# Start of a two-layer flamingo kernel: the first token group's chain and the linear weights ahead, keys and projection weights inside rounds 2 to 4

## The chip, the cores and the metric

One core of a Trainium2 chip runs one program. The metric is the device time of an execution in microseconds (us). One more execution was taken with the hardware profiler; its rows are what is read here. Engines: TensorE (PE; its weight loads are PEld), VectorE (DVE), ScalarE (ACT), GpSimd (POOL) and SyncE (SP), which only issues DMAs.

## The reference, cut to what matters

x is 4 x 2048 tokens of 512 values (8192 tokens), ctx 4 x 77 of 512. All in float32.

```
x = x + tanh(g) * memory(ctx, layernorm(x))     # shifted tokens; 19 "compressed" rows per batch:
                                                # conv_w (4 taps, stride 4) over 76 normed rows of x[1024:1100]
x = x + tanh(g) * (mxq(layernorm(x)) @ mxq(w).T + b)     # blocks of 32, 6-bit grid
x = x + tanh(g) * attention(layernorm(x), keys = D * relu(ctx @ U.T), values = ctx, key mask)
x = x + tanh(g) * experts(layernorm(x))         # router over 8 experts, capacity 1280, relu MLP 512-2048-512
```

The compressed rows enter as the tokens of the last quarter tile of group 1 of each batch. Key mask, keys, values and the router's logits of the context are made once, before they are used.

## The kernel before

Tokens are worked in 16 groups of 512 (4 tiles of 128 rows). A software pipeline of six stages runs over them: in round t the call `body(*groups(t))` on every engine has z = t, a = t-1, b = t-2, c = t-3, d = t-4, e = t-5, each a group's number or None. z: statistics and scale of the first layer norm (`moments("a")`, then `a_m`, `a_sc`, `nb` on VectorE; GpSimd scales `xs` at L1128). a: GpSimd adds `xs` to `X` (L1101), second statistics (L1660), ScalarE normalises to `n1` (L1198), VectorE quantises to `q8` (L1857 to L1869), GpSimd multiplies back (L1112) and adds `gbias` to `X` (L1121), TensorE turns the tiles (`turn_quantised`, L1413), ScalarE and VectorE split them into a high and a low part (`xdT_hi`, `xdT_lo`). b: the linear product with `wd_hi`, `wd_lo` (`linear`, L1405), its addition (L1717), turned tiles of X. c: projection with `uw_hi`, `uw_lo` (L1483), logits, product with the keys (`p_cs`). d: softmax and attention, router. e: slots and stores. Every float32 product is three passes over high and low parts.

Rounds 0 to 5 are written out, rounds 6 to 15 are a loop on the engines that have one, the rest is written out again. The expert stage follows, and its code isn't touched.

The order on each engine is that of its program; the waits on semaphores `k_dve`, `k_act`, `k_pe` go by the place of a step in the lists `DVE_STEPS`, `ACT_STEPS` and `PE_STEPS` (L287 to L303). Preparations: `xc` (76 rows of each batch) is normed and turned (`xcT`), the four taps of `conv_w` are multiplied (L1589), `comp` is stored in `comp_d` and read back as part of group 1's `xs` (L988). `wf` (linear weights) is quantised by VectorE (L1994 to L2002) and multiplied back by GpSimd (L1165), then turned and split (`wd`). `uf` (key weights) is centred by ScalarE with its row sums (L1365 to L1371), turned and split (`uw`). `cx` (the context) is turned and split (`cxT`), and stored split (`cx_d`). Keys: L1618 on TensorE, three steps a part on VectorE (L2009 to L2014), split (L1388, L2042) and stored (`uq_d`). Logits of the context: L1631.

Before the change all preparations but those of `xc` stand between round 0 and round 1 on TensorE, ScalarE and VectorE. GpSimd does the context's low parts (L1161) and `wf` (L1165) ahead of round 0. SP issues the loads in the order g, xc, four taps, group 0 (`load_group`), biases, wf, uf, cx, small ones; then `comp_d`, group 1, the stores of `cx_d` and `uq_d`, waits for everything (`prepared`, `stored`), and goes on with the keys and group 2. `load_group` waits for the addition L1101 of the group before, since `xs` is one buffer.

Of the kernel before, what the change touches and what calls it, by code (L numbers as in the profile page):

```python
# [18 lines left out]
F32 = mybir.dt.float32  # L19
# [9 lines left out]
P = 128  # L29
# [7 lines left out]
def flamingo_two_layers(nc, x, ctx, kmask, g_xattn, g_ffn, conv_w, conv_b, ffn_w, ffn_b, u_w, d_param,  # L37
# [45 lines left out]
    with top:  # L83
# [154 lines left out]
        with setup:  # L238
# [3 lines left out]
            uf = st("uf", [P, KB, D], F32)  # L242
            us, umean, unm = st("us", [P, KB], F32), st("umean", [P, KB], F32), st("unm", [P, KB], F32)
# [3 lines left out]
            xc = st("xc", [CW, B, D], F32)  # L247
            wq8 = st("wq8", [P, KB, D], FP8)
            xcT = st("xcT", [P, KB, B * CW], F32)
# [11 lines left out]
            zrow = n1[0:1, 1, :]  # L261
            comp = n1[0:B * TC, 0, :]
# [11 lines left out]
            uqf = X[:, 2 * T:3 * T, :].rearrange("p t d -> p (t d)")[:, 0:KB * B * L].rearrange("p (k l) -> p k l", k=KB)  # L274
# [3 lines left out]
            l_gate, l_small, l_wf, l_uf, l_cx, l_xc, l_wr = (sem("l_" + n) for n in  # L278
                                                             ("gate", "small", "wf", "uf", "cx", "xc", "wr"))
# [6 lines left out]

            DVE_STEPS = ["zero", *[f"xst{b}" for b in range(B)], *[f"xmv{b}" for b in range(B)],  # L287
                         *[f"xn{b}" for b in range(B)], "nmask", "ng", "mg", *[f"xcT{k}" for k in range(KB)],
                         "gbias", "kmf", "kfree",
                         "wab", "wsc", "win", "wq8", "comp", *[f"uw{k}" for k in range(KB)],  # L290
                         *[f"cxT{k}" for k in range(KB)], *[f"uq{w}{k}" for k in range(KB) for w in "maf"],
                         *[f"wd{k}" for k in range(KB)], "anyk", "anyi", "anyr", "gx", "kbias", "maskb", "wrc", "wrlo", "cwf", "cwlo",
                         *[f"uqlo{k}" for k in range(KB)]]
            dve_at = {n: i + 1 for i, n in enumerate(DVE_STEPS)}
            PE_STEPS = [*[f"xcT{k}" for k in range(KB)], "comp", *[f"uw{k}" for k in range(KB)],
                        *[f"cxT{k}" for k in range(KB)], "keysum", "wrsum", *[f"uq{k}" for k in range(KB)],
                        *[f"wd{k}" for k in range(KB)], "anyk", "cwr"]
            pe_at = {n: i + 1 for i, n in enumerate(PE_STEPS)}
            ACT_STEPS = ["xln", "xrs", "onesr", *[f"us{k}" for k in range(KB)], "unm", "umean", *[f"uc{k}" for k in range(KB)],
# [33 lines left out]
        def convolved(eng):  # L333

            for s, value in ((k_pe, pe_at["comp"]), (w_comp, 16), (w_init, 48)):
                eng.wait_ge(s, value)
# [1808 lines left out]
```

## Time and profile before

| | us |
|---|---|
| median of 3 runs (lowest, highest) | 2067.8 (2064.79, 2069.31) |
| the profiled execution, its time | 2065.28 |
| its span, first to last instruction | 2063.5 |
| TensorE busy in the span | 1927.6 (93%) |
| VectorE, ScalarE, GpSimd busy | 964.2, 742.2, 757.6 |
| mean granted TensorE clock | 0.97 |

The token stage takes the first 700 us or so of the span, the experts the rest. A busy share is an average over both; what the change touches is the first 170 us, read below row by row. The number behind a row's start is its length or that of the merged pieces; x is their count; in square brackets stands the engine's idle time ahead of it and what ended it. A window's row has its stretch, its length, then busy time and instruction count of PE, PEld, DVE, ACT and POOL, the granted TensorE clock (1.00 is 2.4 GHz, 0.50 is 1.2 GHz), the busy share of the DMA queues and GB/s.

### The profile page before, as it was taken

To read this page: it belongs to the slowest core of one execution; us is meant where nothing else is said; L and a number is where in the kernel's file an instruction comes from. 1 tells how busy PE (TensorE), PEld (TensorE's weight loads), DVE (VectorE), ACT (ScalarE), POOL (GpSimd) and SP (SyncE) were. 2 spreads that over 40 slices of the span, in tenths; PEclk is the share of its full clock that TensorE was granted. 3 is DMA by queue.
4 is the path that set the end of the run, shared out by engine and by line. 5 is a ranking of instruction groups with operands and counts; after the bars stand their busy time and mean duration, and the time that the engine had idled before them with its cause. 6 is when DMAs were issued, how large, how long until landed. Compare 5 with 4: busy or idle time off the path is not lost.

```text
span 2063.5 us, 34727 instructions
## 1 busy us (share of the span) xinstructions
PE 1927.6 (93%) x10956; PEld 1637.0 (79%) x10957; DVE 964.2 (47%) x2254; ACT 742.2 (36%) x1707; POOL 757.6 (37%) x803
## 2 busy tenths in 40 slices
PE   3579999999999739999999999999999999999997
PEld 2467777777777538989889988998898898899986
DVE  3678999999996571423312241224224124122331
ACT  2235666666566531423311141114214114111231
POOL 0456566675664231423311151115215115211340
PEclk9589999999999869999999999999999999999999
DMA  7231453443544381433401152004305115200220
GB/s 199 93 94 42 142 178 119 167 136 125 182 133 161 106 284 31 145 96 94 130 30 30 36 167 66 30 30 153 98 25 173 36 36 168 77 30 30 81 82 11
DMA packets 152268, 208.77 MB, mean 101 GB/s; under 512 B 12830, under 2 KB 78622, under 8 KB 152197
## 3 DMA queue, kind: packets, MB, share of 16 engines
q1 hardware_dynamic: 111125, 114.14, 17.8%
q0 software_dynamic: 15728, 43.38, 7.0%
q10 hardware_dynamic: 25344, 50.33, 6.8%
q8 instruction: 41, 0.67, 0.1%
q14 instruction: 30, 0.25, 0.0%
HBM read 140.98 MB, written 68.37 MB: 101 GB/s over the span
## 4 chain that ended last, share of the span: by engine, by line
PE 78%; DVE 6%; issue 5%; DVEq 1%; DMA 1%; ACT 1%; POOL 1%; SPq 0%; ACTq 0%; POOLq 0%
PE bank L788 25%; PE bank L796 24%; PE bank L1483 7%; PE bank L1405 6%; PE bank L756 6%; PE bank L736 6%; PE bank L1455 1%; DVE x2T_lo L1803 1%; PE bank L714 1%; PE bank L745 1%; DVE xdT_lo L1803 1%; DMA stage<-in_L_ffn_W_dram 1%; PE bank L1413 1%; DVE up_lo L1794 1%; DVE a_m L1899 0%
## 5 line engine op out<-in xcount | busy, mean ns | idle before, releaser
L896 DVE SCALAR_TENSOR_TENSOR hT_lo<-bank,hT_hi 128x256 fp32r<-128x256 f32 x352 | 149.2, 424 | 676.9 <-ACT hT_hi L664 676.9
L664 ACT ACTIVATE hT_hi<-bank 128x256 fp32r<-128x256 f32 x352 | 134.9, 383 | 753.9 <-PE bank L788 753.9
L788 PE MATMUL bank<-inT_hi,w_hi 128*128 128x256 f32 x1408 | 399.7, 284 | 0.6 <-DVEq L944 0.6
L788 PE MATMUL bank<-inT_hi,w_lo 128*128 128x256 f32 x1408 | 400.0, 284 | 0.0
L788 PE MATMUL bank<-inT_lo,w_hi 128*128 128x256 f32 x1408 | 396.7, 282 | 0.0
L796 PE MATMUL bank<-w_hi,hT_hi 128*128 128x512 f32 x704 | 280.8, 399 | 0.0
L796 PE MATMUL bank<-w_lo,hT_hi 128*128 128x512 f32 x704 | 277.9, 395 | 0.0
L788 PEld LDWEIGHTS bank<-inT_lo,w_hi 128*128 128x128 f32 x1408 | 266.3, 189 | 14.5
L796 PE MATMUL bank<-w_hi,hT_lo 128*128 128x512 f32 x704 | 277.6, 394 | 0.0
L788 PEld LDWEIGHTS bank<-inT_hi,w_hi 128*128 128x128 f32 x1408 | 266.0, 189 | 13.9 <-DVEq L944 1.0
L788 PEld LDWEIGHTS bank<-inT_hi,w_lo 128*128 128x128 f32 x1408 | 265.2, 188 | 0.0
L497 POOL TENSOR_TENSOR w_lo<-stage,w_hi 128x512 fp32r<-128x512 f32 x112 | 163.4, 1468 | 104.4 <-ACT w_hi L624 104.2
L502 POOL COPY idx_t<-slots 128x2 int32 x23 | 4.2, 184 | 537.5 <-PE bank L714 524.3
L796 PEld LDWEIGHTS bank<-w_hi,hT_lo 128*128 128x128 f32 x704 | 132.2, 188 | 31.9
L796 PEld LDWEIGHTS bank<-w_hi,hT_hi 128*128 128x128 f32 x704 | 132.7, 189 | 17.3
L796 PEld LDWEIGHTS bank<-w_lo,hT_hi 128*128 128x128 f32 x704 | 132.9, 189 | 15.9
L861 DVE TENSOR_TENSOR w_lo<-stage,w_hi 128x512 fp32r<-128x512 f32 x128 | 119.0, 943 | 0.0
L1405 PE MATMUL bank<-wd_hi,xdT_hi 128*128 128x512 f32 x256 | 105.1, 411 | 4.7 <-DVE xdT_lo L1803 2.7
L1483 PE MATMUL bank<-x2T_hi,uw_hi 128*128 128x512 f32 x256 | 106.0, 414 | 1.0 <-DVE rpe L1739 1.0
L1090 POOL TENSOR_SCALAR y<-x,y_sc,y_nb 128x512 f32<-128x512 f32 x64 | 49.4, 785 | 141.7 <-DVE y_nb L1764 141.6
L1405 PE MATMUL bank<-wd_hi,xdT_lo 128*128 128x512 f32 x256 | 101.2, 395 | 0.0
L1405 PE MATMUL bank<-wd_lo,xdT_hi 128*128 128x512 f32 x256 | 101.0, 395 | 0.0
(314 smaller groups left out, 3830.5 us busy)
## 6 DMA issues: line engine op xcount, KB each, us to landing
stage<-in_L_ffn_W_dram SPq DMA_DIRECT2D x256, 256.0 KB, 3.2
X<-in_x_dram SPq DMA_DIRECT2D x16, 1024.0 KB, 5.5
t_d<-tt ACTq DMA_DIRECT2D x16, 1024.0 KB, 4.4
x_d<-x ACTq DMA_DIRECT2D x16, 1024.0 KB, 6.7
out_dram<-y ACTq DMA_DIRECT2D x16, 1024.0 KB, 8.4
xs<-in_x_dram SPq DMA_DIRECT2D x16, 768.0 KB
cw_a<-in_L_xattn_conv_w_dram SPq DMA_DIRECT2D x2, 1024.0 KB, 17.8
cw_b<-in_L_xattn_conv_w_dram SPq DMA_DIRECT2D x2, 1024.0 KB, 19.9
```

What stands on the lines that cost most here:

```text
L497: pool.tensor_tensor(w1_lo[:, :, fs], w1_block(f), w1_hi[:, :, fs].bitcast(F32), ALU.subtract).then_inc(e_split[f % RING], 1)
L664: act.activation(hT_hi[:, f % 4, :], hb[f % 4][:, 0:CN], ACT.Relu).then_inc(e_hh, 1)
L736: last = pe.matmul(first_bank[q % 2][:, :], l[:, k, :], r[:, k, qs], start=(n == 0), stop=(n == 3 * KB - 1))
L756: last = pe.matmul(unit_acc[:, :], l[:, q % 2, f, :], r[:, q * FQ + f, :], start=(q == 0 and n == 0), stop=(q == NF - 1 and n == 3 * FQ - 1))
L788: last = pe.matmul(hb[f % 4][:, 0:CN], l[:, k, fs], r[:, k, :], start=(n == 0), stop=(n == 3 * KB - 1))
L796: last = pe.matmul(acc[i][:, :], l[:, f % 4, js], r[:, f, :], start=(f == 0 and n == 0), stop=(f == FB - 1 and n == 2))
L861: dve.tensor_tensor(w2_lo[:, f, :], w2_block(f), w2_hi[:, f, :].bitcast(F32), ALU.subtract).then_inc(e_split[f % RING], 1)
L896: dve.scalar_tensor_tensor(out=hT_lo[:, f % 4, :], in0=hb[f % 4][:, 0:CN], scalar=0.0, in1=hT_hi[:, f % 4, :].bitcast(F32), op0=ALU.max, o ...
L1090: pool.tensor_scalar(y[:, j:j + 1, :], x3[:, ds((g % 2) * T + j, 1), :], y_sc[:, j:j + 1], y_nb[:, j:j + 1], ALU.mult, ALU.add).then_inc(g ...
L1405: last = pe.matmul(dst, l, r, start=(n == 0), stop=(n == len(terms) - 1))
L1483: last = pe.matmul(u_banks[h % 2][:, :], l, rows_t, start=(k == 0 and n == 0), stop=(k == KB - 1 and n == 2))
L1803: dve.tensor_tensor(lo[:, :, j * P:j * P + P], banks[j % len(banks)][:, :].rearrange("p (k i) -> p k i", k=KB), hi[:, :, j * P:j * P + P]. ...
```

## The change

Loads: xc is read in two pieces (rows 0 to 63, 64 to 75), then tap 0, group 0, tap 1, wf, tap 2, uf, tap 3, the biases with a semaphore of their own (`l_bias`), cx in two pieces, the small ones. Group 2 is fetched right behind group 1, group 3 behind the stores of context and keys. TensorE: the turned linear weights `wd` stand between taps 2 and 3; `uw` behind `comp`; `cxT` (three banks instead of four) between rounds 1 and 2; keys inside round 2, ahead of the turned tiles of group 1; the context's logits inside round 3. VectorE: `wf` after round 0; `gbias`, `comp` and the `wd` low parts inside round 1; mask, `uw` and `cxT` between rounds 1 and 2; key steps inside round 2, their low parts and the small steps behind it; `cwf` inside round 3. In round 1 the first statistics of group 1 come behind the turned tiles. ScalarE: row sums of `uf` ahead of round 1; `wd`, centring and `uw` inside it. GpSimd: rounds start at once; `wf` inside round 1 behind the addition to X, the context's low parts inside round 2. Buffers: `comp`, `xcT`, `wq8`, `uqf` lie in parts of `X` that are free so long. The blanket waits `convolved`, `prepared` and `stored` are gone, single ones take their place. `first_moments` and `first_scale` are the two pieces that stood in VectorE's body before. The core of the diff, banks and list orders left out:

```diff
+            def load_taps(r):
                 half_r = (cw_a, cw_b)[r // (RATE // 2)]
                 sp.dma_start(half_r[:, r % (RATE // 2), :, :], cwv[r, :, :, :]).then_inc(l_cw[r], 16)
+
+            for s0, s1 in ((0, P // 2), (P // 2, CW)):
+                sp.dma_start(xc[s0:s1, :, :], x[:, HALF + s0:HALF + s1, :].rearrange("b s d -> s b d")).then_inc(l_xc, 16)
+            load_taps(0)
             load_group(0, 0)
-            sp.dma_start(fb_raw[:, :], row(ffn_b).broadcast_to([P, D])).then_inc(l_small, 16)
-            sp.dma_start(cb_raw[:, :], row(conv_b).broadcast_to([P, D])).then_inc(l_small, 16)
+            load_taps(1)
             sp.dma_start(wf[:, :, :], ffn_w.rearrange("(k p) i -> p k i", p=P)).then_inc(l_wf, 16)
+            load_taps(2)
             sp.dma_start(uf[:, :, :], u_w.rearrange("(k p) i -> p k i", p=P)).then_inc(l_uf, 16)
-            sp.dma_start(cx[:, :, :], ctx.rearrange("b l d -> l b d")).then_inc(l_cx, 16)
+            load_taps(3)
+            sp.dma_start(fb_raw[:, :], row(ffn_b).broadcast_to([P, D])).then_inc(l_bias, 16)
+            sp.dma_start(cb_raw[:, :], row(conv_b).broadcast_to([P, D])).then_inc(l_bias, 16)
+            for l0, l1 in ((0, P // 2), (P // 2, L)):
+                sp.dma_start(cx[l0:l1, :, :], ctx[:, l0:l1, :].rearrange("b l d -> l b d")).then_inc(l_cx, 16)
...
+            for r0, r1 in ((0, P // 2), (P // 2, B * TC)):
+                sp.dma_start(comp_d[r0:r1, :], X[r0:r1, 3 * T, :]).then_inc(w_comp, 16)
+            sp.wait_ge(w_comp, 32)
             load_group(0, 1)
+            load_group(0, 2)
             sp.wait_ge(k_cxlo, B)
...
+            sp.wait_ge(k_act, act_at[f"uqhi{KB - 1}"])
             sp.wait_ge(k_dve, dve_at[f"uqlo{KB - 1}"])
             sp.dma_start(uq_d.rearrange("b p c -> p b c"),
                          uq_hl[:, :, :, :, :].bitcast(F32).rearrange("p b w k l -> p b (w k l)")).then_inc(w_uq, 16)
-            prepared(sp)
-            stored(sp)
+            sp.wait_ge(w_cx, 16)
+            sp.wait_ge(w_uq, 16)
             load_keys(0)
-            load_group(0, 2)
+            sp.wait_ge(w_init, 48)
             load_group(0, 3)
...
+            def weight_dequantised():
+                pool.wait_ge(k_dve, dve_at["wq8"])
...
+                pool.wait_ge(k_dve, dve_at["gbias"])
+
+            body(*groups(0))
+            body(*groups(1), beside=weight_dequantised)
+            body(*groups(2), beside=context_low)
+            pool.wait_ge(w_init, 48)
+            for t in range(3, STEPS - 1):
...
+            def centred_and_linear():
+                for k in range(KB):
+                    act.wait_ge(k_pe, pe_at[f"wd{k}"])
+                    act.activation(wd_hi[:, k, :], bank[bank_of[f"wd{k}"]][:, :], ACT.Copy).then_inc(k_act, 1)
+                for k in range(KB):
+                    act.activation(uf[:, k, :], uf[:, k, :], ACT.Identity, bias=unm[:, k:k + 1]).then_inc(k_act, 1)
+                act.wait_ge(k_pe, pe_at["comp"])
+
+            def projection_high():
+                for k in range(KB):
+                    act.wait_ge(k_pe, pe_at[f"uw{k}"])
+                    act.activation(uw_hi[:, k, :], bank[bank_of[f"uw{k}"]][:, :], ACT.Copy).then_inc(k_act, 1)
+
+            body(*groups(1), beside=(centred_and_linear, projection_high))
...
+            body(*groups(2))
...
+            body(*groups(3))
...
+                if r == RATE - 1:
+                    pe.wait_ge(k_wdq, KB)
+                    for k in range(KB):
+                        transposes(f"wd{k}", [(slice(n * P, n * P + P), wf[:, n, k * P:k * P + P]) for n in range(KB)])
                 pe.wait_ge(l_cw[r], 16)
...
+            pe.wait_ge(k_dve, dve_at["wd1"])
+            body(*groups(1))
+            pe.wait_ge(l_cx, 32)
+            for n in range(CXN):
+                pe.wait_ge(k_dve, dve_at[("wd2", "wd3", "uw0")[n]])
...
+            def keys():
...
+            def context_logits():
...
+            body(*groups(2), beside=keys)
+            body(*groups(3), beside=context_logits)
...
+                if beside is not None:
+                    beside()
+                opening = isinstance(a, int) and a == 0
+                if not opening:
+                    first_moments()
                 turned_rest(q_banks, xdT_hi, xdT_lo, a, 0, a_bh, v_bl)
                 turned_rest(q_banks, xdT_hi, xdT_lo, a, 1, a_bh, v_bl)
                 up_rest(2)
...
+                if not opening:
+                    first_scale()
                 up_rest(3)
                 turned_rest(q_banks, xdT_hi, xdT_lo, a, 2, a_bh, v_bl)
                 turned_rest(q_banks, xdT_hi, xdT_lo, a, 3, a_bh, v_bl)
+                if opening:
+                    first_moments()
+                    first_scale()
...
+            def compressed_and_linear():
+                dve.wait_ge(l_bias, 32)
+                step("gbias", dve.tensor_scalar(gbias[:, :], fb_raw[:, :], gates[:, 2:3], None, ALU.mult))
+                dve.wait_ge(k_pe, pe_at["comp"])
+                step("comp", dve.tensor_tensor(comp, bank[7][0:B * TC, :], cb_raw[0:B * TC, :], ALU.add))
+                for k in range(KB):
+                    low_part(f"wd{k}", wd_lo[:, k, :], wd_hi[:, k, :])
+
+            body(*groups(1), beside=compressed_and_linear)
+            dve.wait_ge(l_small, 32)
+            step("kmf", dve.tensor_copy(kmf[:, :], km[:, :]))
+            after("kmf")
+            step("kfree", dve.tensor_scalar(kfree[:, :], kmf[:, :], -1.0, 1.0, ALU.mult, ALU.add))
+            for k in range(KB):
+                low_part(f"uw{k}", uw_lo[:, k, :], uw_hi[:, k, :])
+            for n in range(CXN):
+                low_part(f"cxT{n}", cx_turned(cxT_lo, n), cx_turned(cxT_hi, n))
...
+            def keys():
+                for h in range(KB):
+                    dve.wait_ge(k_pe, pe_at[f"uq{h}"])
...
+            body(*groups(2), beside=keys)
...
+            def context_logits():
+                dve.wait_ge(k_pe, pe_at["cwr"])
...
+            body(*groups(3), beside=context_logits)
```

## Rows read from the trace of the kernel before

**Rows 1.** Windows: busy and count per engine, granted clock, DMA share, GB/s

```profile
0.00:20.00 20.00, 0.00 (x0) 0.01 (x1) 3.39 (x11) 3.29 (x6) 2.32 (x20) 1.00 0.84 209
104.00:108.00 4.00, 3.35 (x8) 2.70 (x9) 1.10 (x2) 0.00 (x0) 4.00 (x5) 0.50 0.14 48
200.00:240.00 40.00, 40.00 (x209) 31.37 (x208) 37.36 (x107) 26.19 (x64) 28.17 (x29) 1.00 0.40 132
```

**Rows 2.** Timeline of TensorE: taps, context logits, first linear product of round 4

```profile
25.07 8.55 PE L1589 MATMUL bank<-cw_a,xcT 128*76 128x512 f32 x16 [0.57 <-DVE xcT L1985]
...
78.67 0.30 PE L1631 MATMUL bank<-wr_hl,cxT_hi 128*77 128x16 f32 x1 [2.89 <-DVE wr_hl L2035]
...
82.72 0.28 PE L1631 MATMUL bank<-wr_hl,cxT_lo 128*77 128x16 f32 x1
...
167.62 0.39 PE L1405 MATMUL bank<-wd_hi,xdT_hi 128*128 128x512 f32 x1
```

**Rows 3.** Timeline of GpSimd: dequantisation, scale, additions of groups 0 to 2

```profile
63.56 4.06 POOL L1165 TENSOR_TENSOR wf<-wq,wsc 128x512 f32<-128x512 fp8e4 x4
67.60 3.15 POOL L1128 TENSOR_SCALAR xs<-xs,a_sc,nb_a 128x512 f32<-128x512 f32 x4
70.92 5.19 POOL L1101 TENSOR_TENSOR X<-X,xs 128x512 f32<-128x512 f32 x4 [0.17 <-issue]
...
108.28 5.02 POOL L1101 TENSOR_TENSOR X<-X,xs 128x512 f32<-128x512 f32 x4 [0.17 <-issue]
...
137.34 5.04 POOL L1101 TENSOR_TENSOR X<-X,xs 128x512 f32<-128x512 f32 x4 [0.17 <-issue]
```

**Rows 4.** Timeline of SP: issue of group 1's compressed rows

```profile
77.03 3.75 SPq L988 DMA_DIRECT2D xs<-comp_d  x1
```

**Rows 5.** Timeline of ScalarE: row sums of uf, centring, group 0 normalised

```profile
42.52 0.63 ACT L1365 ACTIVATE uf<-uf 128x512 f32<-128x512 f32 x1 [7.55 <-DMA uf<-in_L_xattn_U_w_dram]
...
45.35 2.56 ACT L1371 ACTIVATE uf<-uf,unm 128x512 f32<-128x512 f32 x4
...
88.88 2.92 ACT L1198 ACTIVATE n<-X,nb_b,rs_b 128x512 f32<-128x512 f32 x4 [0.23 <-DVE nb_b L1670]
```

**Rows 6.** Windows as rows 1, four stretches of the load phase

```profile
20.86:33.83 12.97, 11.28 (x33) 5.96 (x34) 5.69 (x15) 0.00 (x0) 0.00 (x0) 1.00 1.04 336
6.00:15.00 9.00, 0.00 (x0) 0.00 (x0) 0.00 (x0) 0.00 (x0) 0.00 (x0) 1.00 1.04 224
16.50:22.00 5.50, 0.08 (x1) 0.11 (x2) 4.80 (x14) 0.50 (x2) 0.00 (x0) 1.00 1.05 387
36.00:45.00 9.00, 4.49 (x11) 1.92 (x9) 0.00 (x0) 2.48 (x8) 0.00 (x0) 1.00 0.43 101
```

**Rows 7.** Timeline of VectorE: statistics and scale, wf, keys, their low parts, q8

```profile
31.40 2.47 DVE L1660 BATCH_NORM_STATS2 st_a<-xs 128x6 f32<-128x512 f32 x4 [6.39 <-DMA xs<-in_x_dram]
...
35.29 0.15 DVE L1902 SCALAR_TENSOR_TENSOR nb_a<-mv_a,a_m 128x4 f32<-128x4 f32 x1
...
45.78 2.27 DVE L1994 TENSOR_REDUCE wab<-wf 128x64 f32<-128x2048 f32 x1
...
48.91 2.29 DVE L2002 TENSOR_TENSOR wq<-wf,win 128x2048 fp8e4<-128x2048 f32 x1
...
65.76 0.54 DVE L2009 TENSOR_SCALAR X<-bank,umean 128x308 f32<-128x308 f32 x1 [7.29 <-PE bank L1618]
...
73.37 0.38 DVE L2014 TENSOR_SCALAR X<-X,dp 128x308 f32<-128x308 f32 x1
...
83.66 1.64 DVE L2042 TENSOR_TENSOR uq_hl<-X,uq_hl 128x308 fp32r<-128x308 f32 x4
...
93.49 2.50 DVE L1869 TENSOR_TENSOR q<-n,i 128x512 fp8e4<-128x512 f32 x4
```

**Rows 8.** Waits of SP: engine, line, releaser: us in total, times, longest

```profile
SPq L347 <- DMA cx_d<-cx_hl: 10.5, 1, 10.5
...
SPq L98 <- DMA comp_d<-n: 2.9, 1, 2.9
```

More of the change, by code:

```diff
@@ L291, in flamingo_two_layers @@
[L291 to L293 removed]
+                         "wab", "wsc", "win", "wq8", "gbias", "comp", *[f"wd{k}" for k in range(KB)], "kmf", "kfree",
+                         *[f"uw{k}" for k in range(KB)], *[f"cxT{n}" for n in range(CXN)],
@@ L1332, in body @@
                 quantised_hi(3)
+                if beside[1] is not None:
+                    beside[1]()
+                if z is not None and opening:
+                    rstd("a", z)
                 for j in range(T):
@@ L1555, in body @@
                 turn_logits()
+                if beside is not None:
+                    beside()
                 turn_quantised(0)
@@ L1616, in _ @@
+            def keys():
+                pe.wait_ge(k_act, act_at["onesr"])
+                pe.wait_ge(k_dve, dve_at[f"cxT{CXN - 1}"])
                 for k in range(KB):
-                    for n, (a, c) in enumerate(((uw_hi, cxT_hi), (uw_hi, cxT_lo), (uw_lo, cxT_hi))):
-                        last = pe.matmul(bank[bank_of[f"uq{h}"]][:, 0:B * L], a[:, k, hs], c[:, k, :],
-                                         start=(k == 0 and n == 0), stop=(k == KB - 1 and n == 2))
+                    for c in (cxT_hi, cxT_lo):
+                        last = pe.matmul(bank[bank_of["keysum"]][:, 0:B * L], onesr[:, :], c[:, k, :],
+                                         start=(k == 0 and c is cxT_hi), stop=(k == KB - 1 and c is cxT_lo))
@@ L1628, in _ @@
-            for b in range(B):
-                for k in range(KB):
-                    for part in (cxT_hi, cxT_lo):
-                        last = pe.matmul(cwr_bank[:, b, :], part[:, k, b * L:b * L + L], wr_hl[:, k, :],
-                                         start=(k == 0 and part is cxT_hi), stop=(k == KB - 1 and part is cxT_lo),
-                                         skip_group_check=True)
-            last.then_inc(k_pe, 1)
-            body(*groups(1))
-            prepared(pe)
-            for t in range(2, STEPS):
+                pe.wait_ge(l_wr, 16)
@@ new lines, in context_logits @@
+            def context_logits():
+                for b in range(B):
+                    for k in range(KB):
+                        for part in (cxT_hi, cxT_lo):
+                            last = pe.matmul(cwr_bank[:, b, :], part[:, k, b * L:b * L + L], wr_hl[:, k, :],
+                                             start=(k == 0 and part is cxT_hi), stop=(k == KB - 1 and part is cxT_lo),
+                                             skip_group_check=True)
+                last.then_inc(k_pe, 1)
```

276 lines of the change are left out of this document (118 added, 158 removed).

## The prediction

> **What bounds the kernel now.** I read the busy time by stretch first. In a full round the TensorE is busy 40.00 of 40.00 us at the full clock [rows 1]. From there on the order of work is unchanged by the edit, and nothing in it is tied to an absolute time, so it can only start earlier or later as a whole. The question is therefore when the first full round starts: the TensorE begins the linear product of group 2, which opens round 4, at 167.62 us [rows 2]. Second, the chain before it. The rounds cannot start before GpSimd turns to the tokens: it does the context's low parts and then the weight dequantisation (63.56 to 67.62) first, then scales group 0's tokens (67.60) and adds them to X (70.92 to 76.11) [rows 3], though their statistics were there long before. Group 1's tokens are fetched only after that addition: the third piece is issued at 77.03 [rows 4]. So each of rounds 1 to 3 is a loop of latencies (load, statistics, GpSimd scale 3.2, add 5.2, statistics, normalise, quantise, turn), with one addition per round, ending at 76.1, 113.3 and 142.4 [rows 3], and the TensorE is idle in much of it. Third, the load phase: all engines wait for DMA until about 42.5, when the key weights land and ScalarE starts on them [rows 5].
>
> **The loads.** They are put in order of need, and xc and cx are cut at partition 64. In the old order the aggregate was 224 GB/s from 6 to 15 us with xc in flight, 387 after it, 336 over the middle, and 101 at 0.43 of the queues' time over 36 to 45, where cx is the tail [rows 6]. Up to and with uf the new order holds 608 + 3 x 1024 (taps 0 to 2) + 1024 (xs) + 1024 (X) + 1024 (wf) + 1024 (uf) = 7776 KB, 7.96 MB. About 2.3 MB go by 15 us (the old rate from some 4.5 us on); 5.6 MB at 336 GB/s take 16.8, so 31.8, and I add 1.2 for landing: **uf at 33**, against 42.5. Bounds: 31 at 387 GB/s, 36 if the slow start lasts longer. By the same count wf lands at 27, tap 2 at 30, tap 3 at 36, the group-0 tokens at 18 and their X at 21. The Trainium skill (DMA: Bandwidth & Descriptors, "Why a DMA increments its semaphore by 16 and not by 1") says that a transfer runs on the largest number of engines up to 16 that divides its outer dimensions; 76 rows give 4 engines and 77 give 11, while 64 give 16. The tail's share of 0.43 leans that way. If the rule were void, xc would land about where it did, and the sum below would not move, since uf sets it.
>
> **Group 0.** Its statistics, scale and X addition take place at about 18 to 30 (scale 3.2, addition 5.2 [rows 3]), beside the wait for wf and uf. VectorE then does the weight quantisation, 45.78 to 51.20 before, so 5.4 [rows 7]: 27 to 32.4, and group 0's second statistics, about 3 more. ScalarE's row sums and means of uf take 42.52 to 45.35 = 2.8 [rows 5], and they stand ahead of round 1 on its queue: 33 + 2.8 = 35.8 is later than VectorE's 35.4, so uf is what ends last. Add 0.9 for rstd and shift: normalising starts at 36.7. From its start to the end of q8 it was 88.88 to 95.99 = 7.1 [rows 5, 7]: **q8 done at 43.8**, against 95.99. The wait of GpSimd for gbias costs 0.5, with the dequantised tiles of n1 queued behind it.
>
> **Compressed memory and group 1.** comp follows on VectorE, at 45.0, if the TensorE has tap 3 by then: dequantisation 32.4 + 4.1 = 36.5 [rows 3], four wd transposes about 3, a tap 4.3 (half of 8.55 [rows 2]) = 43.8. It would be 48 to 50 at the low clock. Then the store, 2.9 [rows 8] plus 0.3, and the fetch of group 1: in the old run from the end of the addition (76.11) the third piece's issue ran to 80.78 [rows 3, 4], and I take 7 us with the landing (5 to 9): **xs of group 1 at 55.2**. This is a new wait on VectorE's queue, with uw_lo, cxT_lo and round 2 behind it; the TensorE's cxT of the last bank waits too. Statistics, rstd and scale took 31.40 to 35.44 = 4.0 for group 0 [rows 7], GpSimd 3.2 and 5.1, and some 0.5 between them: addition done at **68** against 113.3 [rows 3], 45 earlier. Splits of uw and cxT (about 4 us of VectorE) lie beside GpSimd's 8 and cost nothing; without that cover they would cost those 4.
>
> **Round 2.** The first linear product starts after uw_lo 0, at about 62, and its first tile at the low clock (8 records of 512 columns in 4 us, 0.5 granted [rows 1]) ends at 67; statistics of group 1 thus end at 70.6, not 69, the fourth tile at 75.4. Reduction and q8 need 6 more: **82**, against 125, 43 earlier. Now the keys: 65.76 to 73.75 on VectorE, 8.0 [rows 7], ahead of group 2's statistics and of every low part of the turned tiles. The TensorE makes them from 75.4 to 85, so they overlap and are fed in time. Of the 8, about 5 to 6 count in the end, since the statistics and scale of group 2, which used to run beside GpSimd's bias addition and were slowed by it, now come after it. Scale done at 94.4, GpSimd 3.2 and 5.1: addition of group 2 done at **102.6** against 142.4 [rows 3], 39.8 earlier. Bounds of this step: 4 to 9 lost.
>
> **Round 3.** Key low parts (1.64 [rows 7]) and about ten mask steps of 128 x 16 and less, together an estimated 3.4, stand before round 3 on VectorE. They lie partly beside GpSimd's addition (8 us with the scale), but the low parts of the turned tiles fill most of that, and the linear product again begins at the low clock, which puts group 2's statistics behind it by 2 to 3. I take 4.8 lost (2 to 8): 35 left. The context logits take 78.67 to 83.00 = 4.3 on the TensorE [rows 2], ahead of the turned tiles, and VectorE's reduction of them stands ahead of group 3's statistics; here the TensorE is busy without a gap, so all of it counts. **30.6 left; round 4 opens at 137.0** instead of 167.62. The key store is issued at about 102. In the old run it went out behind the context store, for which alone SP waited 10.5 [rows 8]; alone, and as large (1232 KB each), I take 8 (4 to 17), so group 3's tokens, now behind it on SP, land near 118 (114 to 127), against a need at 127. Hidden, just so at the upper end. The removed waits (convolved, prepared, stored) save nothing: they stood after their work.
>
> **The clock.** The window 0 to 20 shows the full clock granted with no matmul in it, and 104 to 108 the low one, 1.2 GHz, after an idle stretch of the TensorE [rows 1]. The Trainium skill (TensorE: Matmul & The Clock Gate, "What's actually happening") has the throttled state as the default after idling. By that rule, which speaks against this change because it spreads the TensorE's preparations over waits, all taps run at half speed. That is rival B.
>
> **Sum.** Profiled execution: span 2063.5, time 2065.3, so 1.8 lies around it; 2065.3 - 30.6 = 2034.7. The median of the three runs is 2.5 above the profiled one; with half of that, **2036**.
>
> **Rivals.** A, more is gained: loads run at 387 GB/s (uf at 31), the keys cost 4 and the store is quick: 2 + 2 + 3 more, 2029; down to 2023 if group 1's fetch takes 5 and the uw, cxT and mask steps are all covered. For it: the 387 [rows 6]. Against it: the same table's slow start, whose cause no row shows.
> B, low clock in the preparations: three taps behind each other cost 4.3 more each [rows 2], the wd transposes 3; comp comes at 51 instead of 45, and the first linear products lose 2 to 5 more. 8 to 12 of the gain go: 2044 to 2048. Against it: the window 0 to 20 has 1.00 granted with the TensorE idle throughout, and the old taps followed at 0.53 a record [rows 1, 2]; for it: new gaps of 2 to 3 us between taps that wait for DMA.
> C, a new wait takes the place of the old one: group 1's fetch after comp, or group 3's behind the key store. The first decides at once, 1 us per us above 55.2; with landing at 62 it is 2043. The second decides from 127 on; with the store at 17 and the fetch slowed by the X load 5 to 8 are lost: 2042.
> D, no change: the round trips only move, that is, round 4 still opens at 165 to 170. Groups 1 to 3 would have to lose 30 us; [rows 3] show 37 us of addition-to-addition time between groups 0 and 1, and 29 between 1 and 2. I don't see it. 2065.
> E, slower: the TensorE stays at the low clock from round 2 until the first full round. Its work there is about 250 records (two groups' linear products 96, keys and key sums 56, projection and logits 56, the rest turned tiles), at 0.19 us each (40 us for 209) 48 us; at the low clock it doubles (0.43 to 0.5 a record there [rows 1]). Of 48 us more some 12 go into idle time: 2036 + 36 = 2072. It decides once more than 31 + 12 of the 48 are run at the low clock, less it is only B. Against it: the old run had the same kind of gaps and the low clock at 104 to 108, and yet opened round 4 62 us later.
>
> **Chances.** Forecast (2028 to 2041): 0.55. A (below 2028): 0.13. B and C with gains of 4 to 24 (2041 to 2061): 0.24. D: 0.04. E: 0.04. The range 2023 to 2053 leaves out D, E, and the ends of A and B. A measurement of this kernel tells 0.2%, 4.1 us, from no change: faster 0.92, same 0.04, slower 0.04.
>
> **What would show it.** Right: uf's row sums start near 33; the addition of group 1 ends near 68 and of group 2 near 103 on GpSimd; VectorE waits some 4 us for group 1's tokens, and never for group 3's; keys stand between q8 and the statistics of group 2; the linear product of group 2 opens at 137; everything after has the old spacing. Wrong: uf later than 36; a granted clock of 0.5 in the taps; a DMA as what ended the wait for group 3's statistics; or full rounds that are no longer 40 of 40.

## The result and the profile after

The changed kernel takes 2040.3 us (median of 4 runs, 2039.7 to 2042.1) against 2066.7 of the kernel before, run beside it: ratio 0.9872, 95% interval 0.9858 to 0.9886. It is faster by 26.4 us; 2036 was forecast, so the time is 4.3 us longer, inside the forecast range of 2028 to 2041 and near its upper end. The profiled execution took 2040.0, with a span of 2038.2 (25.3 less than before) and a mean granted clock of 0.977 for 0.970.

Timeline of TensorE: start, length, engine, line, what; in brackets the idle time ahead and what ended it. These lines answer to [rows 2].

```profile
16.70 8.63 PE L1625 MATMUL bank<-cw_a,X 128*76 128x512 f32 x16 [0.57 <-DVE X L2036]
25.91 3.73 PE L1625 MATMUL bank<-cw_b,X 128*76 128x512 f32 x8 [0.59 <-DMA cw_b<-in_L_xattn_conv_w_dram]
35.08 3.68 PE L1606 MATMUL bank<-ident,wf 128*128 128x128 f32 x16 [5.44 <-POOL wf L1174]
38.55 4.47 PE L1625 MATMUL bank<-cw_b,X 128*76 128x512 f32 x8
...
128.59 0.23 PE L1667 MATMUL bank<-wr_hl,cxT_hi 128*77 128x16 f32 x1
...
130.83 1.09 PE L1439 MATMUL bank<-ident,n 128*128 128x128 f32 x8
...
142.07 0.51 PE L1431 MATMUL bank<-wd_hi,xdT_hi 128*128 128x512 f32 x1 [1.67 <-DVE cwr L2109]
```

Round 4 opens at 142.07 for 167.62, 25.55 earlier, and this is the whole gain: the addition to X of group 15 ends at 589.4 for 614.8, 25.4 earlier, and the spacing of one group's addition to the next is 37.2 in both traces (two neighbouring groups: 291.1 - 253.9 and 316.8 - 279.6). So the question is again what set 142.07.

Timeline of GpSimd, which answers to [rows 3]: the additions end at 31.0, 75.0, 108.2 and 144.5 for 76.1, 113.3, 142.4 and 172.1, that is 45, 38, 34 and 28 earlier. Each round of the three gives some of the start back.

```profile
24.02 7.00 POOL L1105 TENSOR_TENSOR X<-X,xs 128x512 f32<-128x512 f32 x4 [0.17 <-issue]
30.98 4.05 POOL L1174 TENSOR_TENSOR wf<-X,wsc 128x512 f32<-128x512 fp8e4 x4
...
69.98 5.05 POOL L1105 TENSOR_TENSOR X<-X,xs 128x512 f32<-128x512 f32 x4 [0.17 <-issue]
...
102.67 5.52 POOL L1105 TENSOR_TENSOR X<-X,xs 128x512 f32<-128x512 f32 x4 [0.28 <-POOL xs L1134]
```

Timeline of VectorE, which answers to [rows 7]. The third line holds its largest wait of the first 150 us.

```profile
8.08 2.47 DVE L2019 BATCH_NORM_STATS2 xst<-xc 76x6 f32<-76x512 f32 x4 [6.55 <-DMA xc<-in_x_dram]
16.56 2.46 DVE L1698 BATCH_NORM_STATS2 st_a<-xs 128x6 f32<-128x512 f32 x4
62.52 2.47 DVE L1698 BATCH_NORM_STATS2 st_a<-xs 128x6 f32<-128x512 f32 x4 [12.72 <-DMA xs<-comp_d]
...
84.78 2.50 DVE L1929 TENSOR_TENSOR q<-n,i 128x512 fp8e4<-128x512 f32 x4
...
104.41 4.51 DVE L2083 TENSOR_TENSOR uq_hl<-X,uq_hl 128x308 fp32r<-128x308 f32 x4
...
141.28 0.74 DVE L2109 TENSOR_TENSOR cwr<-cwf,cwr 77x32 fp32r<-77x32 f32 x1 [0.92 <-ACT cwr L1422]
```

What the 12.72 are: the first line is the chain that ended last (start, length, what), the others are windows, with the columns of [rows 1].

```profile
47.29 15.09 DMA xs<-comp_d
...
54.00:57.00 3.00, 0.00 (x0) 0.00 (x0) 0.00 (x0) 0.00 (x0) 0.00 (x0) 0.50 0.78 266
57.00:60.00 3.00, 0.00 (x0) 0.00 (x0) 0.00 (x0) 0.00 (x0) 0.00 (x0) 0.50 0.07 25
60.00:62.50 2.50, 0.00 (x0) 0.00 (x0) 0.00 (x0) 0.00 (x0) 0.00 (x0) 0.50 0.07 25
```

From 57 us on nothing in the core works but the DMA engines, and they at 0.07 of the time of all sixteen and 25 GB/s: about one of the sixteen carries what is left. The fetch of group 1 has pieces of 768 KB (384 rows), 218 KB (109 rows) and 38 KB (19 rows), and X of 1024 KB. This gave the experiments.

### The profile page after: what moved, and what is told of

Same layout as the page of the kernel before. It is cut to its first block, busy times and chain, and to the rows that moved or that the text cites. A ratio compares the mean times of both kernels' runs of the same rounds, so it can differ in the third digit from the quotient of the medians.

```text
span 2038.2 us, 34720 instructions
## 1 busy us (share of the span) xinstructions
PE 1918.6 (94%) x10956; PEld 1629.3 (80%) x10957; DVE 960.5 (47%) x2253; ACT 741.8 (36%) x1706; POOL 760.7 (37%) x803
## 4 chain that ended last, share of the span: by engine, by line
PE 82%; DVE 7%; issue 5%; DMA 2%; DVEq 1%; ACT 1%; POOL 1%; ACTq 0%; SPq 0%; POOLq 0%
PE bank L781 25%; PE bank L789 24%; PE bank L1511 7%; PE bank L1431 7%; PE bank L729 6%; PE bank L749 6%; PE bank L1483 1%; DVE x2T_lo L1841 1%; PE bank L707 1%; PE bank L738 1%; DMA xs<-comp_d 1%; DVE xdT_lo L1841 1%; PE bank L1439 1%; DVE a_m L1860 0%; DVE up_lo L1832 0%
## 6 DMA issues: line engine op xcount, KB each, us to landing
cw_a<-in_L_xattn_conv_w_dram SPq DMA_DIRECT2D x2, 1024.0 KB, 10.8
```

## The experiments

All kernels compute the full reference. Each was run beside the kernel before; the times (in us), and the start of round 4 in the one execution that was profiled:

| kernel | median us | ratio to before (95%) | round 4 opens |
|---|---|---|---|
| changed kernel | 2040.3 | 0.9872 (0.9858, 0.9886) | 142.07 |
| e1_split | 2032.0 | 0.9834 (0.9818, 0.9851) | 134.80 |
| e2_early | 2034.4 | 0.9847 (0.9831, 0.9864) | 135.04 |
| e7_order | 2029.7 | 0.9821 (0.9805, 0.9838) | 130.97 |
| e5_xcwhole | 2048.6 | 0.9908 (0.9892, 0.9925) | 150.71 |
| e6_tapsfirst | 2046.5 | 0.9901 (0.9885, 0.9918) | 149.16 |
| e4_uqlo | 2038.2 | 0.9869 (0.9852, 0.9885) | 140.81 |
| e8_keysact | 2039.7 | 0.9865 (0.9849, 0.9882) | 141.65 |
| e10_keysact_uqlo | 2034.9 | 0.9847 (0.9830, 0.9863) | 137.67 |
| e3_cwlo | 2038.4 | 0.9869 (0.9852, 0.9885) | 141.12 |
| e9_warm | 2040.6 | 0.9875 (0.9859, 0.9892) | 140.75 |
| e11_best | 2021.3 | 0.9779 (0.9763, 0.9795) | 124.11 |
| e12_best_g3 | 2022.6 | 0.9781 (0.9764, 0.9797) | 124.86 |

The intervals are some 3 us to either side, so smaller differences between two of these kernels are not told apart by them; for those I go by the start of round 4 in the trace. That has a scatter too: six of the kernels (the changed one, e3_cwlo, e4_uqlo, e8_keysact, e9_warm, e10_keysact_uqlo) fetch group 1 in the same way, and its statistics start between 61.7 and 62.7 in their traces. About 1 us in the start of round 4 is therefore no effect of an edit by itself.

### Group 1's fetch

**e1_split** cuts the odd piece of every group's fetch; in group 1 its 109 rows become 96 and 13.

```diff
-                sp.dma_start(xs[0:m, T - 1, :], rows(r + shift + G - P, m)).then_inc(s_xs, 16)
+                cut = {1: 96, 3: 48}.get(q, P // 4)
+                for m0, m1 in ((0, cut), (cut, m)):
+                    sp.dma_start(xs[m0:m1, T - 1, :], rows(r + shift + G - P + m0, m1 - m0)).then_inc(s_xs, 16)
```

> Every group's fetch goes in four pieces instead of three: the first piece, of 109 rows in groups 1, of 51 in groups 3 and of 64 in the others, is cut into 96+13, 48+3 and 32+32 rows. In the changed kernel group 1's tokens reach VectorE at 62.5 us, 15.5 us after SyncE issued them, and from 60 to 65 us the DMA engines' share is .06, one engine of sixteen. Theory: the tail is the 109-row piece that one engine carries. Then 96 rows spread, 13 rows are a short tail, the statistics of group 1 start at 54 to 57 and round 4's first matmul comes 5 to 7 us earlier, at 135 to 137; the time is 2033 to 2036. Rival: the compressed rows (19, written to DRAM and read back, not cut here) or the round trip of their store hold the group; then the statistics still start at 61 to 63 and the time stays at 2039 to 2042.

Measured: 2032.0. VectorE's statistics, then the chain that ended last:

```profile
54.20 2.47 DVE L1700 BATCH_NORM_STATS2 st_a<-xs 128x6 f32<-128x512 f32 x4 [4.49 <-DMA xs<-comp_d]
...
47.78 6.29 DMA xs<-comp_d
```

8.3 us earlier, with the same bytes, in one piece more. The theory holds (the time is 1 us better than its range); the 19 rows and their way through DRAM were not what held the group. SyncE's issue of the compressed rows, 4.01 us long in the changed kernel, took 0.25 here: it too had waited behind the piece of 109 rows. The rule behind it was in the prediction for another load. The Trainium skill (DMA: Bandwidth & Descriptors, "Why a DMA increments its semaphore by 16 and not by 1") picks the largest number of engines up to 16 that divides the outer dimensions; by that rule 109 gives one engine and 96 gives sixteen, and the trace agrees, with 0.07 of sixteen engines' time at 25 GB/s behind the 109 rows.

**e2_early** moves everything of group 1 but the 19 rows ahead of the wait (`late=True` leaves these out).

```diff
+            load_group(0, 1, late=True)
             sp.wait_ge(k_dve, dve_at["comp"])
...
-            load_group(0, 1)
+            sp.dma_start(xs[KEEP_A - (HALF - P):P, T - 1, :], comp_d[0:TC, :]).then_inc(s_xs, 16)
```

> Of group 1's fetch, everything but the 19 compressed rows (its 109 other token rows and X) is issued ahead of SyncE's wait for the compressed rows; only the 19 rows follow the store. Theory: VectorE's 12.7 us of idle time ahead of group 1's statistics is the transfer of the large piece, which has no reason to wait. Then the statistics start at 50 to 53, the addition to X of group 1 ends by 65, and round 4's first matmul comes 8 to 10 us earlier; 2030 to 2033. First rival: the store and read back of the 19 rows, on one engine, take over, so that the statistics start at 56 to 58 and the gain is 4 to 6 us (2034 to 2036). Second rival: what is late next (GpSimd's scales and additions, TensorE's first linear layer at 68 with its clock low before it) takes nearly all; round 4 opens within 2 us of 142 and the time is 2038 to 2042.

Measured: 2034.4, the time of the first rival (its statistics at 56 to 58 are missed). The large piece is out of the way, and yet the statistics start at 54.34. SyncE's waits (engine, line, releaser: us in total, times, longest), then windows of the stretch before and during this wait:

```profile
SPq L1049 <- DMA comp_d<-X: 6.2, 1, 6.2
```

```profile
40.00:42.00 2.00, 2.00 (x6) 1.04 (x5) 1.58 (x3) 1.84 (x4) 0.21 (x1) 1.00 0.95 337
42.00:44.00 2.00, 2.00 (x15) 1.50 (x15) 1.12 (x2) 0.00 (x0) 2.00 (x3) 1.00 0.24 84
...
46.00:48.00 2.00, 0.96 (x8) 0.82 (x9) 1.29 (x2) 0.95 (x3) 2.00 (x2) 1.00 0.07 25
```

SyncE waited 6.2 us for the store of the compressed rows, for 1.4 in the changed kernel. I first put this down to X's 1 MB, now in flight ahead of the store, and the expectation of the next run says so. The windows show something else. The bulk of the loads was through by 43, and the store was issued at 43.59; from 46 on the engines are at 0.07 and 25 GB/s again, the mark of the 109 rows, which are not cut in this kernel. What fits is a store held up by the queue of one engine: the odd piece, and X's share on that engine behind it. That is read from the windows and not shown by a run, and how the 6.2 us split between the two is not measured. **e7_order** takes both away: it has both edits, and X behind the compressed rows:

> Both ideas on group 1's fetch together, with one more: the 109-row piece is cut as in the kernel with four pieces (96+13), all of the group's token rows are issued ahead of SyncE's wait for the compressed rows, and X follows only behind the 19 compressed rows. Where only the rows and X went early, the store of the compressed rows took 6.2 us, with X's 1 MB in flight, and the statistics of group 1 started at 54.3. Theory: the store was held up by X; without it the store takes about 2.5 us, the 19 rows some 3, and the statistics start as soon as VectorE is free, at 49.6 to 51. TensorE's and GpSimd's work of round 1 ends at 49.5 and 50.8, so round 4's first matmul comes 3 to 4.5 us ahead of the 134.8 of the kernel with four pieces: 130.5 to 132; 2029 to 2031. Rival: the 19 rows' way through DRAM, on one engine, takes the same 6 us however empty the queues are; the statistics start at 53 to 54 and the time is 2032 to 2034.

Measured: 2029.7, the theory in time and in the start of round 4; its reason, that X alone held the store, is not shown by it, since the odd piece is cut in it as well.

```profile
50.33 2.47 DVE L1704 BATCH_NORM_STATS2 st_a<-xs 128x6 f32<-128x512 f32 x4 [0.75 <-DMA xs<-comp_d]
...
130.97 0.50 PE L1437 MATMUL bank<-wd_hi,xdT_hi 128*128 128x512 f32 x1 [1.69 <-DVE cwr L2115]
```

SyncE's wait for the store is 1.4 us again, and of VectorE's 12.72 us of waiting 0.75 are left. From the changed kernel to this one the statistics come 12.2 earlier, round 4 11.1, the span 10.8. In e1_split it is 8.3, 7.3 and 5.2: there round 4 had the low clock soon after its start, as these windows show, and gave some back.

```profile
136.00:138.00 2.00, 2.00 (x6) 1.58 (x5) 0.00 (x0) 0.00 (x0) 0.00 (x0) 0.50 0.35 48
138.00:140.00 2.00, 2.00 (x10) 1.57 (x10) 0.27 (x1) 0.00 (x0) 0.00 (x0) 0.75 0.88 327
```

### The loads

**e5_xcwhole** undoes the cut of xc alone (`for s0, s1 in ((0, CW),)`), **e6_tapsfirst** the order alone (`load_taps(0)` to `load_taps(3)` ahead of `load_group(0, 0)`).

> Of the change, only the cut of the compressed segments' load is undone: the 76 rows come in one piece and not in 38 and 38; the order of the loads stays that of the changed kernel. In the kernel before VectorE started on these rows at 16.5, in the changed one at 8.1. Theory: with one piece, on a few of the sixteen engines, the rows arrive at 14 to 16 again; VectorE makes them before group 0's statistics, which then start at 21 to 24 for 16.6, and all that follows shifts by 5 to 7 us: 2045 to 2047. Rival: the pieces behind it gain from the engines that it leaves free, and group 0's chain has slack up to the linear weight at 23.2: 2040 to 2042.

> The order of the loads is that of the kernel before: all four convolution taps, then group 0's tokens, the linear weight, the projection weight; all else is as in the changed kernel. Theory: in the changed kernel the linear weight (VectorE starts on it at 23.2, after 2.6 us of idle time) and group 0's tokens (16.6) set round 1; with 2 MB of taps ahead of the tokens, 5 to 6 us at 387 GB/s, group 0's statistics start at 21 to 23 and the linear weight lands at 28 to 29; the normalised tokens come 4 to 5 us later, tap 3 waits for nothing more than before, and the time is 2043 to 2045. Rival: the last tap matmul and the projection weight, whose place in the queue hardly moves, set the compressed rows and with them group 1's fetch; the time stays at 2040 to 2041.

(The change cuts xc into 64 and 12 rows; the 38 and 38 of the first text are a slip.) Measured: 2048.6 and 2046.5; both theories, each some 1.5 us above its upper end. The first two lines are of e5_xcwhole, the third is of e6_tapsfirst:

```profile
16.37 2.47 DVE L2019 BATCH_NORM_STATS2 xst<-xc 76x6 f32<-76x512 f32 x4 [14.84 <-DMA xc<-in_x_dram]
...
24.84 2.46 DVE L1698 BATCH_NORM_STATS2 st_a<-xs 128x6 f32<-128x512 f32 x4
```

```profile
23.58 2.47 DVE L1696 BATCH_NORM_STATS2 st_a<-xs 128x6 f32<-128x512 f32 x4 [6.84 <-DMA xs<-in_x_dram]
```

Against 16.56 group 0's statistics come 8.3 and 7.0 later, and the addition of group 0 ends 8.3 and 7.0 later too (39.3, 38.0 for 31.0); the medians are 8.3 and 6.2 up. There is next to no slack behind group 0's statistics: what they lose, the kernel loses. Nearly a third of the change's 26.4 hangs on the cut of a 608 KB load.

### VectorE and GpSimd beside each other

**e4_uqlo** moves the keys' low parts into round 3, just ahead of VectorE's last linear addition, away from GpSimd's addition of group 2.

```diff
+                if between is not None:
+                    between()
                 add_linear(3)
```

> The low parts of the projected keys (one VectorE subtraction of 4.51 us at 104.4 in the changed kernel, 1.64 us in the kernel before) stand inside round 3, just ahead of VectorE's third linear addition, in place of ahead of the first. Theory: the operation is long because GpSimd runs an addition of the same kind beside it, and there it holds round 3's linear additions up. In its new place VectorE has some 2 us to spare and GpSimd is quiet: it lasts 1.6 to 1.7 us, and round 4 opens 3 to 4.5 us earlier; 2036 to 2037.5. Rival 1: the length is the operation's own in this layout; it stays 4.5 and costs 2 to 3 us at its new place: 2038.5 to 2040. Rival 2: the stores of the keys and group 3's fetch behind them come later by some 10 us, land at about 137 or later, and hold round 3's last statistics: slower, 2041 to 2046.

Measured: 2038.2, round 4 at 140.81: 1.3 us gained, and not the 3 to 4.5. The operation itself did as the theory says (1.65, first line). The rest went into what the second line shows, group 3's tokens, which now stand behind the keys' store, and into GpSimd's addition, which ended at 108.1 as before: two of the small steps now stand beside it, and took 0.85 and 1.23 us (`anyr`, `gx`) for 0.16 and 0.23. So rival 2 holds in part.

```profile
113.27 1.65 DVE L2107 TENSOR_TENSOR uq_hl<-X,uq_hl 128x308 fp32r<-128x308 f32 x4
...
129.87 2.47 DVE L1698 BATCH_NORM_STATS2 st_a<-xs 128x6 f32<-128x512 f32 x4 [1.19 <-DMA xs<-in_ctx_dram]
```

**e8_keysact** gives four of the keys' twelve operations to ScalarE.

```diff
-                    step(f"uqm{h}", dve.tensor_scalar(uqf[:, h, :], bank[bank_of["keysum"]][:, 0:B * L], umean[:, h:h + 1],
-                                                      None, ALU.mult))
-                    after(f"uqm{h}")
+                    dve.wait_ge(k_act, act_at[f"uqs{h}"])
...
+                for k in range(KB):
+                    act.activation(uqf[:, k, :], bank[bank_of["keysum"]][:, 0:B * L], ACT.Copy,
+                                   scale=umean[:, k:k + 1]).then_inc(k_act, 1)
```

> The product of the keys' column sums with the projection's means (four operations of 0.53 us on VectorE inside round 2) is made by ScalarE, which stands idle there for 4.8 us; VectorE's part of the keys, 87.2 to 94.8 in the changed kernel, shrinks to some 5.4 us. Theory: VectorE is busy without a gap from 81.4 to 100 in round 2, so what the keys take on it counts in full: 2.1 to 2.4 us less, round 4's first matmul at 139.7 to 140, 2037.5 to 2038.5. Rival: GpSimd's scale and addition of group 2 or TensorE's transpositions stand beside the keys and take their place: less than 0.8 us is gained, 2039.5 to 2041.

Measured: 2039.7, round 4 at 141.65: the rival. But its reason is another one. The keys shrank from 7.6 to 4.1 us (87.63 to 91.7) and round 3's first product came 3.0 earlier, at 99.58. Then:

```profile
96.41 1.19 DVE L1870 TENSOR_TENSOR a_sc<-a_m,ng 128x4 f32<-128x4 f32 x1
...
101.26 5.97 DVE L2089 TENSOR_TENSOR uq_hl<-X,uq_hl 128x308 fp32r<-128x308 f32 x4
...
109.21 0.65 PE L1439 MATMUL bank<-wd_hi,xdT_hi 128*128 128x512 f32 x1 [3.92 <-DVE X L1763]
```

VectorE ran into all of GpSimd's addition (101.18 to 106.90). Its four subtractions and GpSimd's four additions took turns, at some 1.5 us for each of the four pairs; TensorE stood 3.9 us and then had the low clock. **e10_keysact_uqlo** has both edits:

> Two edits together on the changed kernel, each of which has run alone: the keys' four mean products on ScalarE, and the subtraction for the keys' low parts inside round 3. With ScalarE's products alone round 3 opened 3.0 us earlier (99.6 for 102.6), but that subtraction then lasted 5.97 us for 4.51, TensorE stood 3.9 us and fell to the low clock, and round 4 opened only 0.4 us earlier. Theory: the gain was real and was lost in the contention of VectorE and GpSimd; with the subtraction away from GpSimd's addition the two gains add up to more than their sum, round 3's second statistics end at 108 to 109 (113.1 in the changed kernel), round 4 opens at 137 to 139; 2035 to 2036.5. Rival: GpSimd's addition to X of group 2 itself, or group 3's tokens, issued behind the store of the keys and needed 15 us after it, hold the round in their turn: round 4 opens at 140 or later, 2037.5 to 2039.

Measured: 2034.9, round 4 at 137.67: 4.4 earlier, where the two edits alone gave 1.3 and 0.4. In this execution group 1's fetch came 0.8 earlier; even without that the two together give more than their sum. The theory holds, and the 4.51 us of the low parts were contention.

How it works is seen in the smallest operations: a_sc, 128 x 4 values, takes 0.16 us where GpSimd is idle. In e8_keysact it started at 96.41, 0.11 us behind one of GpSimd's additions (96.30 to 97.58), took 1.19 and ended with it. Not every operation is slowed. In the changed kernel group 2's statistics, which read one tile in SBUF, took 2.46 us beside GpSimd's additions as elsewhere, and the key step with an operand in PSUM (the memory that TensorE writes to; here `bank`) 0.48. The Trainium skill (SBUF — State Buffer, "SBUF: two separate sides") has VectorE and GpSimd share a pair of ports, which VectorE needs for an operation with two inputs in SBUF or in a two-port mode, and which whoever comes first holds for its whole instruction; by that rule such an operation waits for the rest of GpSimd's running instruction, whatever its own size, and this trace agrees.

### The waits and the clock

**e3_cwlo** moves TensorE's wait for `cwlo` into round 4, to its use, and ScalarE's part of the step into round 3.

> TensorE's wait for the low part of the context logits' weight, which stands ahead of round 4, stands at the first use of that weight inside round 4, and ScalarE makes the high part inside round 3 and not behind it. Theory: in the changed kernel TensorE's 1.67 us of idle time ahead of round 4 is this wait and nothing else; round 4's first matmul then comes 1.7 us earlier, at 140.4, and the time is 2038.5. Rival: the wait only covers for VectorE's or ScalarE's own lateness, and the same idle time turns up a few instructions later in round 4: 2040.

Measured: 2038.4, as the theory has it; but round 4 opens at 141.12 and not 140.4. The wait of 1.7 us is gone (no idle time ahead of round 4), the context logits had begun 0.4 us earlier (128.21 for 128.59), and the clock took 1.1 back: a low spell stands right behind the context logits where the changed kernel has none.

```profile
130.00:132.00 2.00, 2.00 (x18) 1.98 (x18) 1.37 (x4) 0.71 (x2) 2.00 (x3) 0.77 0.00 0
132.00:134.00 2.00, 2.00 (x6) 1.54 (x5) 2.00 (x8) 0.86 (x3) 2.00 (x2) 0.50 0.00 0
```

TensorE's work just before it, the context logits, is the same in both. So a gain of 1 to 2 us in these rounds can be taken or given by where such a spell falls; what decides it the rows don't show.

**e9_warm** keeps TensorE busy while it has nothing to do.

```diff
+                if n == 2:
+                    pe.wait_ge(v_bl, T)
+                    for _ in range(70):
+                        pe.matmul(bank[2][:, :], xdT_hi[:, 0, 0:P], wd_hi[:, 0, :], start=True, stop=True)
```

> TensorE, idle from 49.5 to 67.5 in the changed kernel and granted half its clock from about 51 to 71, makes 70 matmuls of 128x512 in this gap (some 16 us at 0.23 us each) whose results nobody reads; nothing else differs. Theory: the low clock costs round 2's first linear layer 1.7 us (six matmuls of 0.63 against 0.39, and their starts 0.43 against 0.23 us apart); with the clock high when round 2 starts, VectorE's third and fourth additions come 1.5 to 2 us earlier, and the time is 2038 to 2039. Rival: the end of GpSimd's addition to X of group 1 at 75.0, which the second statistics wait for, covers the first linear layer whatever the clock: gain under 0.5 us, 2039.8 to 2041. Third: TensorE's dummy work delays the transposition of the context behind it: up to 1 us slower.

Measured: 2040.6. The clock was high as meant (0.39 us a record from 67.08 on, where the changed kernel has 0.63 from 68.01), and the first rival took it: VectorE's statistics wait for GpSimd's addition, tile by tile.

```profile
71.96 0.70 DVE L1702 BATCH_NORM_STATS2 st_b<-X 128x6 f32<-128x512 f32 x1 [0.39 <-POOL X L1105]
73.21 0.69 DVE L1702 BATCH_NORM_STATS2 st_b<-X 128x6 f32<-128x512 f32 x1 [0.55 <-POOL X L1105]
74.46 0.69 DVE L1702 BATCH_NORM_STATS2 st_b<-X 128x6 f32<-128x512 f32 x1 [0.55 <-POOL X L1105]
```

Round 4 opens 1.3 earlier, of which 0.7 is the fetch's own scatter (61.81 for 62.52), and the medians show no gain. The low clock in round 2 thus costs some 0.6 us, if anything.

### All of it

> All edits that helped, in one kernel: the order and cut of group 1's fetch (2029.7 alone), the wait for the context logits' low part at its use, the keys' mean products on ScalarE, the low parts of the keys inside round 3. If they add up, round 4 opens at 124 to 126 and the time is 2023 to 2025. Rival: group 3's fetch, which stands behind the store of the keys and their load, sets round 3: its tokens need some 15 us from the subtraction, so VectorE waits for them by 2 to 5 us, and the time is 2025.5 to 2028.

> As the kernel with all edits, but SyncE issues group 3's fetch right behind the issue of the keys' store, ahead of its wait for that store and of the keys' load. If group 3's tokens set round 3 in the kernel with all edits, this one is 2 to 4 us faster, at 2022 to 2024, and VectorE doesn't wait for them; if they don't, the two are equal within 0.5 us.

Measured: 2021.3 and 2022.6. **e11_best** is 45.4 us under the kernel before and 19.0 under the changed one, and better than its theory; group 3's fetch doesn't set round 3 there (VectorE starts its statistics at 113.72 without a wait), and e12_best_g3, which only brings this fetch forward, is no faster. Its chain that ended last, and TensorE at round 4:

```profile
45.69 4.17 DMA xs<-comp_d
...
124.11 0.40 PE L1448 MATMUL bank<-wd_hi,xdT_hi 128*128 128x512 f32 x1
```

## Why the prediction was right, and where it was wrong

**The frame held.** That only the opening of round 4 counts, and that it moves all that follows as a whole: 25.55 there, 25.4 at group 15, 25.3 in the span. (TensorE is busy 39.5 of 40 us from 200 to 240, not 40.00; the spacing of the groups is unchanged.)

**The loads.** Right in size, wrong in what they set. ScalarE starts on uf at 28.60, not 33: the queues gave 387 GB/s from 15 us on and 273 from 10 to 15, where I had used 336 and the old slow start. But the sum did not use these 4.4 us, since "uf is what ends last" was wrong: normalising began at 34.09 (36.7 forecast), released by VectorE's statistics, behind the weight quantisation. The step that failed outright is the sentence that without the Trainium skill's rule "xc would land about where it did, and the sum below would not move, since uf sets it". e5_xcwhole has xc where it was, and everything moves by 8.3. I had looked for the load that lands last; what counts is the first one on VectorE's queue, because the statistics of group 0 stand behind it there.

**Group 0 and comp.** q8 done at 41.20 (43.8), comp started at 43.06 (45.0): 1.9 early. It wasn't q8 that set comp, as the sum has it, but what stood there as a condition: VectorE waited 1.47 us for TensorE, whose tap 3 ended at 43.0 (43.8 forecast), with the wd transposes at the low clock. That chain starts with GpSimd: the addition of group 0, then wf (4.05), the transposes, tap 3. The addition took 7.00 for 5.19. Three of its four instructions took 1.26 to 1.27, the fourth 3.33, beside VectorE's product over the whole weight (128x2048, from 27.18, 2.70 for 2.29): 2 us of contention on the path that set comp.

**Group 1's fetch: the miss.** From its first issue (46.47) to the statistics it took 16.0 us, and 7 (5 to 9) was put down, read off the time at which the third piece's issue ended. No row of before shows when this fetch landed: VectorE took it up at 95.90, late for other reasons, so the trace bounded it only by 19.7 from above. The end of an issue is no landing. And that rule of the Trainium skill, which I had applied to the 76 and 77 rows, I did not apply to the 109 of this load. Since comp was 1.9 early, the statistics started at 62.52 for 55.2, 7.3 late. It is rival C's first mechanism at its size ("with landing at 62 it is 2043"), though the rate was less than 1 us per us: e7_order gives 0.9. With the fetch about where I had put it the rest of the sum is 1 to 2 us too high: in e1_split and e2_early the statistics start at 54.2 and 54.3, round 4 opens at 134.8 and 135.0 for 137.0, and the time is 2032 and 2034 for 2036.

**Round 2.** q8 ended at 87.28 for 82, 5.3 late, so this part went 2.0 better than put; the low clock that I had counted in it lay behind GpSimd's addition (e9_warm). The keys took 7.6 for 8.0, and the addition of group 2 ended 5.6 late (108.19 for 102.6): the 5 to 6 that were to count are confirmed by their sum, within 0.3. The reason given for the discount is not: GpSimd's work does lie beside them. One and the same key step takes 0.79, 1.09 and 1.30 us where it starts behind one of GpSimd's instructions, and 0.38 where it starts just ahead of one (94.45 for 94.54).

**Round 3.** The low parts' 1.64 became 4.51, 2.9 us of contention that the sum put at nought (e4_uqlo, e10_keysact_uqlo). TensorE's wait for `cwlo` ahead of round 4, 1.7 us, has no term in the sum (e3_cwlo). The context logits were over-priced: 4.3 was read off rows at the low clock [rows 2], and with the clock high they take 2.24 (128.59 to 130.83), 2.1 less. These three are 2.5 late; with the 5.6 that is 8.1, and round 4 came 5.1 late (142.07 for 137.0). The other 3.0 I put, by what remains, to the 4.8 for the start of round 3, of which the low clock was to be 2 to 3: its first products ran at the high clock, and the low one came later (mean 0.70 over 110 to 115). How much that cost was not measured. The keys' store took 4.3 for 8, and group 3's tokens were hidden, as put. That the time is as near as it is, is in part luck: the terms that came out too small (5.6 up to the addition of group 2, 4.6 in round 3) met terms that were 5.1 too large.

**Rivals.** A's fast loads and quick store came true and brought nothing, since uf set nothing. B is refuted for the taps: the clock stood at full speed from 0 to 30 us, and only the wd transposes and part of tap 3 ran low. D and E did not happen.

## What to carry to other kernels

A transfer's cost can hang on its row count: before a load is moved onto the path, look at the factors of its rows, and try to cut a prime count into a multiple of sixteen and a rest (here 109 into 96 and 13). When a small transfer is late, look at what else its engines still have to carry. What counts among several loads need not be the one that lands last; it can be the one that heads an engine's program. When a VectorE operation with two inputs in SBUF (or one that scales a tile in SBUF, as the key step does) stands beside GpSimd's work, its price in a new place is that of its neighbour, and two edits that fail alone for this reason may pay together.

## What the runs showed that was not expected

- 218 KB in 109 rows left about one DMA engine at work alone for the last 5.5 us of a fetch, and cost the group 8.3 us against the same bytes in 96 + 13 rows.
- SyncE waited 1.4 us for a DRAM store of 76 rows with the queues empty, and 6.2 behind an uncut load of 109 rows and one of 1 MB, though the engines together were at 0.07 of their time for part of it (46 to 48 us).
- A VectorE operation of 0.16 us took 1.19 beside a GpSimd addition of 128x512, and such an addition of 1.27 took 3.33 beside a VectorE product over 128x2048.
- The clock was granted in full for the first 30 us with TensorE idle until 13.55, and fell to half between 30 and 35 (mean 0.85), in a gap of 5.4 us without a matmul.
